# More identity transposes on TensorE in the early pauses of a two-layer attention kernel

## The reference

```
# layer 0, for each of the 32 batches (channels x length), 8 heads of 16 channels
q, k = Wq y + bq, Wk y + bk          # y = ctx
v = Wv x + bv
scores = q k^T / sqrt(128);  attn = softmax(scores)        # over channels
o = Wo (attn v) + bo + x
x = groupnorm of one group(o) * gn_w + gn_b
# layer 1, 32 query heads, 8 key heads, every weight with a rank-16 addition
q = x Wq + 2 x Aq Bq;   k, v = the same from ctx
context = softmax(q k^T / sqrt(32)) v
out = x + (context Wo + 2 context Ao Bo)
```

## Time and profile before

| | |
|---|---|
| median of 3 executions | 1324.83 us (1324.82, 1324.83, 1327.98) |
| the profiled execution | 1328.18 us, span 1326.2 us |
| mean granted clock of TensorE | 0.988 |
| TensorE busy | 1299.6 us, 98% of the span |
| DVE, ACT, POOL busy | 69%, 62%, 12% |
| DMA | 240 GB/s over the span |

### The profile page before, as it was taken

One profiled execution on the slowest core, in us unless ns is written; L12 is line 12 of the kernel. 1 busy time (PEld: TensorE's weight loads), 2 busy tenths in 40 slices (PEclk: granted clock), 3 DMA queues, 4 the chain that ended last, 5 costly groups with the idle time before them and its releaser, 6 DMA issues.

```text
span 1326.2 us, 22899 instructions
## 1 busy us (share of the span) xinstructions
PE 1299.6 (98%) x6824; PEld 1022.6 (77%) x6824; DVE 918.8 (69%) x2037; ACT 828.3 (62%) x2899; POOL 153.1 (12%) x117
## 2 busy tenths in 40 slices
PE   6899999999999999999999999999999999999999
PEld 5677888878788888888888888767767767766767
DVE  4576666666656777777777775687776776766666
ACT  3566666666632777777757776766666666654441
POOL 2344333223210000000000002400000000000000
PEclk7899999999999999999999999999999999999999
DMA  8468777889867887878777888999999899988882
GB/s 283 134 209 289 264 269 255 291 282 299 268 218 211 232 230 227 236 224 227 227 215 224 238 231 273 269 255 250 257 254 263 239 252 258 251 233 230 231 223 93
DMA packets 191785, 318.67 MB, mean 240 GB/s; under 512 B 21136, under 2 KB 85904, under 8 KB 190960
## 3 DMA queue, kind: packets, MB, share of 16 engines
q1 hardware_dynamic: 191664, 317.22, 82.1%
HBM read 232.20 MB, written 84.93 MB: 239 GB/s over the span
## 4 chain that ended last, share of the span: by engine, by line
PE 95%; DVE 2%; issue 1%; ACT 1%; DMA 1%; POOL 0%; SPq 0%; DVEq 0%; POOLq 0%; ACTq 0%
PE bank L647 26%; PE bank L697 23%; PE bank L528 14%; PE bank L718 8%; PE bank L751 5%; PE bank L762 5%; PE bank L600 3%; PE bank L514 2%; PE bank L618 2%; PE bank L503 1%; PE bank L633 1%; PE bank L555 1%; PE bank L572 1%; PE bank L562 1%; PE bank L560 1%
## 5 line engine op out<-in xcount | busy, mean ns | idle before, releaser
L979 ACT ACTIVATE bank<-bank,negs 128x128 f32<-128x128 f32 x1024 | 347.5, 340 | 174.8 <-DVE negs L1254 174.6
L647 PE MATMUL bank<-hT,wq 128*128 128x512 f32 x1488 | 390.3, 400 | 0.0
L697 PE MATMUL bank<-wo,op 128*128 128x512 f32 (+1 forms) x1356 | 345.8, 393 | 0.3 <-issue 0.3
L647 PEld LDWEIGHTS bank<-hT,wq 128*128 128x128 f32 x1488 | 264.0, 189 | 46.3
L697 PEld LDWEIGHTS bank<-wo,op 128*128 128x128 f32 x1356 | 249.6, 189 | 51.8 <-issue 1.5
L1249 DVE TENSOR_REDUCE maxes<-bank 128x4 f32<-128x512 f32 x256 | 175.8, 687 | 133.4 <-PE bank L718 133.2
L996 ACT ACTIVATE probT<-bank 128x512 f32<-128x512 f32 x256 | 152.0, 604 | 113.5 <-PE bank L751 111.8
L528 PE MATMUL bank<-wkv_hi,yT 128*128 128x512 f32 x512 | 210.4, 430 | 7.8 <-POOL wkv_lo L1535 5.1
L979 ACT ACTIVATION_READ_ACCUMULATOR bank<-bank,negs 128x1 f32 x1024 | 209.7, 205 | 0.0
L718 PEld LDWEIGHTS bank<-k_stack,q_stack 96*128 96x128 f32 x1024 | 150.3, 191 | 16.3 <-issue 0.4
L718 PE MATMUL bank<-k_stack,q_stack 96*128 96x128 f32 x1024 | 147.3, 266 | 0.2 <-DMA q_stack<-q_dram 0.2
(11 more groups left out here) (146 smaller groups left out, 1563.7 us busy)
## 6 DMA issues: line engine op xcount, KB each, us to landing
q_stack<-q_dram SPq DMA_DIRECT2D x256, 256.0 KB, 4.0
q_dram<-q_part SPq DMA_DIRECT2D x64, 512.0 KB, 4.1
q_stack<-q_dram SPq DMA_DIRECT2D x256, 128.0 KB, 4.3
yT_in<-in_ctx_turned SPq DMA_DIRECT2D x32, 512.0 KB, 5.0
y_in<-in_ctx SPq DMA_DIRECT2D x32, 512.0 KB, 5.7
x_in<-in_x SPq DMA_DIRECT2D x32, 512.0 KB, 4.3
h_dram<-h_out SPq DMA_DIRECT2D x32, 512.0 KB, 4.3
h_in<-h_dram SPq DMA_DIRECT2D x32, 512.0 KB, 3.6
```

Source lines behind the costliest of these rows:

```text
L647: m = pe.matmul(bank(u % 2).rearrange("p (a n) -> p a n", a=2), wq[:, block, part, c, :], hT[(group + 1) % 2][:, :, of, c, :], start=c == ...
L697: mm = pe.matmul(place[:, columns], op[m][:, of, c, :], wo[m][w][:, c, columns], start=c == 0 and of == 0 and w == 0, stop=c == GROUP - 1 ...
L979: act.activation(part, part, ACT.Exp, bias=negs[:, n % RING, j:j + 1], scale=SCORE1, accum_out=sums[:, score_column(k), g, j:j + 1]).then_ ...
```

## The change

TensorE turns the identity more often: 58 times instead of 22 at the very start, and in four new places: 20 times after `score_product(0)`, 8 times between chunks 5 and 6 of batch 0, 16 times after `mix_product(0)`, and 24 times in batch 1, between chunk 6 and the low-rank product. The last call has a wait of its own, for the first batch's turned keys. That makes 104 more transposes. No other engine has another instruction, another order or another wait.

```
             pe.wait_ge(S["const"], CONST["ident"])
-            keep_on(22)
+            keep_on(58)
...
             score_product(0)
+            keep_on(20)
             kv_products(0, (3, 4))
             n1_product(0)
-            kv_products(0, (5, 6))
+            kv_products(0, (5,))
+            keep_on(8)
+            kv_products(0, (6,))
             mix_product(0)
+            keep_on(16)
             kv_products(0, (7,))
...
                 kv_products(b, (6,))
+                if b == 1:
+                    pe.wait_ge(S["kT"], 1)
+                    keep_on(24)
                 prep_product(unit_of(b))
```

## The result

The changed kernel takes 1322.18 us in the median of 14 executions (1318.35 to 1327.3). The kernel before, executed beside it, takes 1327.3 us (14 executions, 1324.19 to 1330.64). The ratio is 0.996, 95% interval 0.9947 to 0.9974: faster by 0.4%, 5.1 us. The forecast was 1319.7 us, in a range from 1315.5 to 1322.5. The profiled execution of the changed kernel takes 1318.35 us, span 1316.5; before it was 1328.18 and 1326.2. Profile against profile the gain is 9.8 us, nearly twice that of the medians. The experiments first ask what the fills do to the clock, and then where this difference comes from.

A forecast was written before the change was run, and what follows sets the result against it. TensorE's own work was taken as the bound, with low clock in the first 56 us. Five stretches gain 10.2 us, one remaining fall costs 1.7, so 1328.18 - 8.5 = 1319.7 us, range 1315.5 to 1322.5.

The forecast's parts named there:

- The bound and the place: Whole kernel: TensorE, busy 98% of the span, is the bound; the gain lies in the first 56 us and reaches the end.
- Transposes hold the clock: At the start: transposes alone bring TensorE to its upper clock, read from 418 ns falling to 273 ns in the median.
- The slower rival: In all fills: transposes run at 1.2 GHz, the 58 end at 13.9 us, total 1336 us; chance 0.06.
- The legs: Five low-clock stretches in the first 56 us: their work runs at the upper level, gaining 10.2 us in sum.
- for that case 1318.0 us was forecast: Whole kernel, rival: no fall of the clock is left, 1328.18 - 10.2 = 1318.0 us; chance 0.22.
- The fills cost nothing: In the five pauses: the 104 transposes fit and in themselves cost 0.
- 7.7 us from 1.5, end at 9.2: First fill: 58 transposes end at 9.2 us, 0.2 us before the first low-rank product's wait ends at 9.43.
- One of my signs of being wrong, a start after 9.5 us: Behind the first fill: the forecast is wrong if the low-rank products start after 9.5 us; 9.43 was expected.
- The pauses left: Ahead of chunk 0 and batch 1's low-rank product: 1.7 and 1.9 us stay open, near the length that brings falls.
- I take one fall of the two: At the two open pauses: one clock fall, costing 1.7 us, leaves 8.5 us of gain; chance 0.32.
- The evidence that I had for a fall behind 1.3 us: Kernel before: a pause of 1.30 us, followed by half a us more before 31.8, brought the clock down.
- so I read the spread as this same clock: Executions before, two groups 3.2 us apart: attributed to low stretches, so counted from 1328.18 us; rival of another cause 0.10.

The follow-up runs named there:

- number 6: Changed kernel with 12 more transposes before chunk 0, 40 instead of 24 in batch 1, 50 instead of 58 at the start: 1319.14 us, ratio 0.9934 against the kernel before.
- 11: Changed kernel with 12 more transposes before chunk 0, 40 instead of 24 in batch 1, 38 instead of 58 at the start: 1319.14 us, ratio 0.9942 against the kernel before.
- Experiment 4: Changed kernel with 12 more transposes ahead of chunk 0 and 40 instead of 24 in batch 1: 1319.39 us, ratio 0.9938 against the kernel before.
- experiment 12: Changed kernel with fills of 50, 12 (new, before chunk 0), 24, 14, 23 and 40: 1319.81 us, ratio 0.9949 against the kernel before.
- experiment 5: The changed kernel executed again, nothing altered, for its spread: 1322.62 us, ratio 0.9959 against the kernel before.
- experiment 10: Changed kernel with 40 instead of 24 transposes in batch 1, nothing added ahead of chunk 0: 1320.66 us, ratio 0.9949 against the kernel before.
- experiment 1: Kernel before with only the first fill raised from 22 to 58, none of the other four: 1325.65 us, ratio 0.9988 against the kernel before.
- experiment 8: Changed kernel with each later fill halved to 10, 4, 8 and 12, 58 kept: 1322.54 us, ratio 0.9958 against the kernel before.

## Why the prediction was right or wrong

**The bound and the place: right.** In the profiles the whole gain lies ahead of 56 us, and behind it TensorE does what it did before in the same time (compare the last line of the earlier trace rows, 1261.91 of 1270.50 us):

```profile
46.20:1316.50 1270.30, 1261.83 (x6683) 991.74 (x6681) 893.20 (x1986) 805.55 (x2854) 134.94 (x96) 1.00 0.83 241
```

In the two profiles the start of `turn_gram` of batch 2 goes from 55.84 to 46.23, 9.6 us, and the end by 9.7 us. It is carried to the end.

**Transposes hold the clock: right.** The clock rises after nothing but transposes in every profile here, at 5.2 us in the profile after. The slower rival is excluded. The Trainium skill's rule in "TensorE: Matmul & The Clock Gate", Part 4, that they don't engage the upper clock, does not hold on this trace for fp32 transposes.

**The legs: right, each within 0.3 us.** Forecast and measured gain, by the same start and end in the chain (the first leg from 9.43 in both, so its measured gain is after the overrun of the fill; from its own start at 9.86 it is 1.9):

| leg before | forecast | measured |
|---|---|---|
| 9.43 to 13.20 | 1.7 | 1.45 (9.43 to 11.75) |
| 15.57 to 22.0 | 2.9 | 2.7 (14.11 to 17.84) |
| 24.72 to 27.82 | 1.3 | 1.25 (20.52 to 22.38) |
| 34.07 to 38.68 | 2.2 | 2.0 (28.62 to 31.26) |
| 50.77 to 55.84 | 2.1 | 2.2 (43.34 to 46.23) |
| sum | 10.2 | 9.6 |

The profiled execution after had no fall, and for that case 1318.0 us was forecast: it took 1318.35. Chunk 0, chunk 3, chunk 7 and the query unit stand 0.4, 0.5, 0.6 and 0.9 us later than forecast (13.7, 20, 28 and 42.4).

**The fills cost nothing: right for four, off for the first.** I had "7.7 us from 1.5, end at 9.2" with the clock rising after 3.0 us. The moment of the rise differs from execution to execution: 4.4, 5.2, 5.8, 6.9, 7.6 us in profiles of these runs. The low-rank products behind the 58 therefore start between 9.35 and 10.78 us. The latest start is 1.4 us behind what POOL's end would have allowed. One of my signs of being wrong, a start after 9.5 us, came: it is 9.62 in the profile after. It was right about this term, which I had put at nothing, and says nothing against the rest. Experiments 6 and 11 show that 50 or 38 do as well.

**The pauses left: right in size, and right as the cause of the falls.** Forecast 0.6, 0.7, 1.0 (from the fills' lengths), 1.7 and 1.9 us; measured 0.52, 0.74, 0.87, 1.45 with 0.35 ahead of it, and 1.88. "I take one fall of the two" is right as a mean: the 25 executions have 11 with one and 6 with two, 0.9 per execution. A price of 1.7 us was 1.6 in the chain and 1.5 to 2.0 between the groups. Experiment 4 takes both pauses away and with them the falls: 22 of 22 executions of numbers 4, 6, 11 and 12 are at 1.000. The evidence that I had for a fall behind 1.3 us was weaker than I read it. The fall at 31.8 us came 0.4 us into the next pause, of 2.67 us, and the same trace has a single pause as long, 1.32 us up to 376.79, where the clock stays at 1.00 (the kernel before, waits from 56 us on: us, times, longest):

```profile
PE bank L600 <- issue: 1.3, 1, 1.3
```

**What was off: "so I read the spread as this same clock".** The forecast was 1319.7 us for one fall and the median is 1322.2, 2.5 us above, 0.3 us inside the range. The executions with one fall have a median of 1322.3 (experiment 5), so it isn't the number of falls. At a mean clock of 1.000 the changed kernel has 1318.35 to 1322.85 us, median 1320.3, where I had put 1318.0. With the 0.999 and 0.997 of the table the sum is short by 2.6 and 2.5 us. So some 2.3 to 2.6 us were missing at every clock, and the clock explains only a part of the spread. The traces show two terms that the sum had at nothing. The first fill runs past its wait, by 0.4 us in one profile and 1.4 in the other. And waits in the second stage vary: experiment 12 has 2.3 us for two loads, of which the profiled execution of before happened to have 0.2. So I counted from an execution slow in its clock and fast in its loads. How the 2.3 us of the median divide between the two was not measured.

The range's upper end, 1322.5, stood for two falls and 1 us of late fill. What filled it was one fall, late fills and late loads, so that the median lies inside it is in part luck. The measured gain, 5.1 us, is less than the 9.6 of the legs for a second reason: the legs are those of a profile with 30.7 us of low clock, and many executions of the kernel before have less. Of 63 of them, beside the experiments, 11 have a mean clock of 0.995 and take 1324.2 us in the median, 12 have 0.988 as the profiled one and take 1329.4. The groups between them are not in strict order (0.990 has 1329.6), so the clock alone doesn't order them.

**What stays open.** Why the clock falls behind a given pause in one execution and not in the next was not isolated: 1.46 us did it in experiment 10, while 2.70 us in experiment 1 and 1.74 us in experiment 8 did not. Why a stack load lands late in one execution is open too, and it was not tried to move these loads. Nor was an execution profiled in which 38 at the start end early.

## What to carry to other kernels

Idle pauses of an engine whose clock follows its activity can be paid twice, once as idle time and once in the work behind them. When cheap filler is put into them, what is left open decides, not what was filled: with 0.9 us or less left of each early pause none of 22 executions fell, with 1.45 and 1.9 us left 17 of 25 did. A filler that overruns its pause is to be counted as work. And when executions of one kernel spread by 5 us, sort them by clock before a sum is made against a single profile. The version to keep here is number 6 or 11, 1319.1 us in both, 3.5 us under the changed kernel where it ran beside it (number 6), and 9.0 and 7.9 us under the kernel before.

## What the runs showed of the hardware

- fp32 transposes of the identity alone bring TensorE from the lower to the upper clock: 418 ns each in the median, then 273. In the profile after, with them in the pauses, the granted clock is 1.00 from 5.2 us to the end.
- The moment at which the clock rises is not tied to the start of the kernel: with the same first instruction at 1.5 us it rose anywhere from 4.4 to 7.6 us.
- At a full clock, one load of `q_stack<-q_dram` (128 KB, 4.2 to 4.5 us in the medians of two profiles from issue to landing) took 5.7 us in one execution, and TensorE waited 1.8 us for it; in another, of a kernel that is the same there, it waited for none. This was about half of the 3.7 us by which the two spans differ.
- A single pause of 1.32 us, up to 376.79 us in the kernel before, left the granted clock at 1.00, one of 1.46 us ahead of 13.86 (experiment 10) was followed by a low stretch from 14.6 to 18.0, and one of 2.70 us ahead of 21.0 (experiment 1) was not.
